# Softmax sums taken before the transposition, values as the stationary side: two attention layers of a four-layer kernel

## The reference, cut to what matters

```
x  = x + attention(q, k, v of norm(x), mask A) @ w_ao + b_ao     # self-attention
x  = x + attention(q of norm(x), k, v of ctx, mask B) @ w_co + b_co   # cross-attention
x  = x + gelu(norm(x) @ w1 + b1) @ w2 + b2                       # MLP, 256 -> 1024 -> 256

def attention(q, k, v, mask):                # 16 heads of 16 features, 64 keys
    scores = q k^T / 4
    scores = scores * mask - 10000 * (1 - mask)
    return softmax(scores) @ v
```

## Time and profile before

| what | us |
|---|---|
| median of 3 runs (lowest, highest) | 1135.61 (1134.04, 1136.98) |
| the profiled execution | 1134.52, of which 1132.7 between its first and last instruction |
| layer 0 and entry, up to the first `probs_T` | 120.8 |
| turn 0 | 68.9 |
| the six turns of the loop | 501.2 |
| turn 7, up to the next block's first matmul (L1620) | 74.2 |
| what follows (last MLP, layer 3) | 367.6 |

### The profile page before, as it was taken

The page is one execution under the profiler, slowest core; times in us unless marked ns, Lnnn a source line. Parts: engine busy times, 40 slices in busy tenths (PEclk is TensorE's granted clock), DMA queues, the critical chain, the costliest instruction groups (busy, mean ns, idle before and its releaser), DMA issues. The chain is left out here.

```text
span 1132.7 us, 23729 instructions
## 1 busy us (share of the span) xinstructions
PE 1030.0 (91%) x9056; PEld 707.2 (62%) x9056; DVE 768.0 (68%) x1517; ACT 517.4 (46%) x996; POOL 440.2 (39%) x387
## 2 busy tenths in 40 slices
PE   7988889999999999999999999998977978889766
PEld 5876666677777777678677677673453453544524
DVE  3655878856766766757757758744566796896854
ACT  4644354572572572662663663541404415314331
POOL 2111444443433433433443433523146356175240
PEclk9989889999999999999999999999989999999988
DMA  8130100001002002103001000300010010010100
GB/s 264 61 98 29 43 2 25 20 2 44 20 2 81 20 2 86 38 2 122 17 4 60 2 19 21 128 2 19 0 38 22 1 38 21 0 40 1 37 1 19
DMA packets 38005, 41.14 MB, mean 36 GB/s; under 512 B 8640, under 2 KB 33536, under 8 KB 37648
## 3 DMA queue, kind: packets, MB, share of 16 engines
q1 hardware_dynamic: 37776, 39.54, 10.9%
q0 software_dynamic: 128, 0.10, 0.1%
HBM read 31.25 MB, written 8.39 MB: 35 GB/s over the span
## 5 line engine op out<-in xcount | busy, mean ns | idle before, releaser
L2106 POOL TENSOR_TENSOR c_rs<-c_st,head_area 128x512 f32<-128x512 f32 x64 | 88.7, 1416 | 96.8 <-DVE c_st L2585 96.0
L787 POOL TENSOR_TENSOR head_area<-head_area,b_self_add 128x1024 f32<-128x1024 f32 x32 | 75.8, 2368 | 114.4 <-DVE head_area L1366 114.4
L1039 PE MATMUL ps<-b_hT_mlp,wl 128*128 128x512 f32 x224 | 107.0, 605 | 0.0
L787 POOL TENSOR_TENSOR head_area<-head_area 128x1024 f32<-128x1024 f32 x32 | 77.1, 2411 | 76.7 <-DVE head_area L1366 76.7
L1053 PE MATMUL ps<-w,b_act_g 128*128 128x256 f32 x448 | 100.9, 381 | 0.0
L1373 DVE TENSOR_REDUCE b_neg_max<-head_area 128x16 f32<-128x1024 f32 x64 | 77.5, 1211 | 34.1 <-POOL head_area L787 34.0
L1208 ACT ACTIVATE head_area<-head_area 128x1024 f32<-128x1024 f32 x64 | 67.9, 1061 | 62.6 <-DVE head_area L1378 62.5
L1213 ACT ACTIVATE head_area<-ps 128x512 f32<-128x512 f32 x128 | 69.8, 601 | 55.6 <-PE ps L986 55.6
L1053 PEld LDWEIGHTS ps<-w,b_act_g 128*128 128x128 f32 x448 | 83.4, 190 | 11.6 <-issue 1.0
L792 POOL TENSOR_TENSOR b_rstd<-b_var,minus_half 128x1 f32<-128x1 f32 x63 | 40.8, 648 | 124.9 <-DVE b_var L1402 124.2
L870 PE MATMUL ps<-head_area,wl 128*128 128x512 f32 x176 | 84.5, 609 | 3.9 <-issue 1.9
(11 more groups left out here) (262 smaller groups left out, 2155.9 us busy)
## 6 DMA issues: line engine op xcount, KB each, us to landing
head_area<-x_mid SPq DMA_DIRECT2D x9, 512.0 KB, 3.8
wl<-in_wl SPq DMA_DIRECT2D x4, 1024.0 KB, 7.0
head_area<-in_ctxT SPq DMA_DIRECT2D x8, 512.0 KB, 3.6
x_mid<-b_x_out SPq DMA_DIRECT2D x8, 512.0 KB, 3.5
area<-in_wc SPq DMA_DIRECT2D x1, 2336.0 KB, 8.2
a_x_in<-in_x SPq DMA_DIRECT2D x16, 128.0 KB, 2.9
a_y_in<-in_ctx SPq DMA_DIRECT2D x16, 128.0 KB, 3.6
w<-in_w SPq DMA_DIRECT2D x2, 1024.0 KB, 9.1
```

What stands on the lines that cost most here:

```text
L787: pool.tensor_tensor(t, t, m.unsqueeze(1).broadcast_to([P, NH, S]), ALU.add).then_inc(add_ok, 1)
L1039: mm = pe.matmul(ps[:, YB + j % 2, :], weight("w1", k, j * P, (j + 1) * P), hT_mlp[:, k, :], start=(k == 0), stop=(k == NC - 1))
L2106: pool.tensor_tensor(rs[:, i % BUFS, :], st[:, i % 3, :], rF[:, i // RS, :], ALU.mult).then_inc(rs_ok, 1)
```

## The change

- `row_sums` is new on DVE: a sum over 64 keys of the exponentials (128x1024) and a reciprocal, tile k + 1 in step k.
- `scale` is new on POOL: the probabilities times the reciprocals, 128x1024, in place; `probs_T` waits for it in place of `exps`.
- `times_v`: the values are the stationary side (128 keys x 32 columns, two heads) and the transposed probabilities move (64 columns). Four pairs of heads write four groups of 32 PSUM partitions. The result comes out transposed. The column of ones is gone (values are 32 wide instead of 34), and with it four memsets on POOL at the start.
- `normalize` (DVE) and `result_T` (PE) are removed.
- The order of a turn is new on PE, ACT, DVE and POOL.

```diff
+            def scale(n, k):
+                t = sc[:, k % 2, :, :, :].rearrange("q f i k -> q (f i) k")
+                pool.wait_ge(inv_ok, tile(n, k) + 1)
+                pool.tensor_tensor(t, t, inv_sum[:, k % 2, :].unsqueeze(2).broadcast_to([P, NH, S]), ALU.mult).then_inc(prob_ok, 1)
...
             def probs_T(n, k, nxt):
                 if k + 1 < TILES or nxt is not None:
                     pe.wait_ge(mul_ok, tile(n, k) + 2)
-                pe.wait_ge(exp_ok, tile(n, k) + 1)
+                pe.wait_ge(prob_ok, tile(n, k) + 1)
...
                 for half in range(2):
                     pe.wait_ge(pT_ok, 2 * tile(n, k) + half + 1)
-                    for i in range(NPAIR // 2):
-                        j = half * NPAIR // 2 + i
-                        for b in range(2):
-                            q = slice(b * S, (b + 1) * S)
-                            mm = pe.matmul(ps[q, CX, j * 2 * VW:(j + 1) * 2 * VW], pT[:, half, i, q], vP[a][:, 2 * p + b, j, :],
-                                           start=True, stop=True)
-                mm.then_inc(v_sum_ps, 1)
-
-            def result_T(n, k):
-                pe.wait_ge(tok_ok, tile(n, k) + 1)
-                for half in range(2):
-                    f = slice(half * P, (half + 1) * P)
-                    mm = pe.transpose(ps[:, CX, f], c_tok[:, f], w["ident"][:, :])
+                    for b in range(2):
+                        q = slice(b * S, (b + 1) * S)
+                        for i in range(NPAIR // 2):
+                            mm = pe.matmul(ps[i * PW:(i + 1) * PW, CX, half * P + b * S:half * P + (b + 1) * S], vP[a][:, 2 * p + b, half * NPAIR // 2 + i, :],
+                                           pT[:, half, i, q], start=True, stop=True)
                 mm.then_inc(c_ps, 1)
...
-            def normalize(n, k):
-
-                dve.wait_ge(v_sum_ps, tile(n, k) + 1)
-                heads = ps[:, CX, 0:NH * VW].rearrange("q (i v) -> q i v", v=VW)
-                dve.reciprocal(inv_sum[:, :], heads[:, :, HD:VW].rearrange("q i v -> q (i v)")).then_inc(inv_ok, 1)
-                dve.wait_ge(inv_ok, tile(n, k) + 1)
-                dve.tensor_tensor(c_tok[:, :].rearrange("q (i d) -> q i d", d=HD), heads[:, :, 0:HD],
-                                  inv_sum[:, :].unsqueeze(2).broadcast_to([P, NH, HD]), ALU.mult).then_inc(tok_ok, 1)
+            def row_sums(n, k):
+                t = sc[:, k % 2, :, :, :].rearrange("q b i k -> q (b i) k")
+                dve.wait_ge(exp_ok, tile(n, k) + 1)
+                dve.tensor_reduce(inv_sum[:, k % 2, :], t, AX, ALU.add).then_inc(sum_ok, 1)
+                dve.wait_ge(sum_ok, tile(n, k) + 1)
+                dve.reciprocal(inv_sum[:, k % 2, :], inv_sum[:, k % 2, :]).then_inc(inv_ok, 1)
...
             maximum(0, 0)
             subtract(0, 0)
             mask(0, 1)
+            row_sums(0, 0)
             turn(0, None, 1)
```

More of the change, by code:

```diff
@@ L34 @@
 NM = ROWS // HD
-VW = HD + 1
+PW = 2 * HD
 DFF = 1024
@@ L191 @@
 N_B_CONST = 4
-N_ZERO = 6
+N_ZERO = 2
 N_C_CONST = 11
@@ L321, in _ @@
                 pool.memset(w[a + "_v"][:, :, :, :], 0.0).then_inc(zero_ok, 1)
-            pool.wait_ge(zero_ok, 2)
-            for a in ("self", "cross"):
-                for odd in range(2):
-                    pool.memset(w[a + "_v"][odd * S:(odd + 1) * S, :, :, odd * VW + HD:odd * VW + VW], 1.0).then_inc(zero_ok, 1)
             pool.wait_ge(zero_ok, N_ZERO)
@@ L743, in _ @@
             store(5, rows[1])
-            sp.wait_ge(v_sum_ps, tile(TURNS - 1, NP))
+            sp.wait_ge(c_ps, tile(TURNS - 1, NP))
             for dst, src in load_c_weights(w, io):
@@ L804, in last_inv_std, with next_scale @@
                     inv_std(prev, TILES - 1)
+            def next_scale(n, k, nxt):
+                if k + 1 < TILES:
+                    scale(n, k + 1)
+                elif nxt is not None:
+                    scale(nxt, 0)
             def next_add_mask(n, k, nxt):
@@ L852, in _ @@
             add_mask(0, 1)
+            scale(0, 0)
             for p in range(NP):
@@ L1130, in turn @@
                 hidden(prev, 7, nxt)
-                last_project(n, 5, prev)
-                result_T(n, 5)
+                last_project(n, 6, prev)
                 probs_T(n, 6, nxt)
@@ L1137, in turn @@
                 next_scores(n, 6, nxt)
-                last_project(n, 6, prev)
-                result_T(n, 6)
                 mlp_out(prev, 0, nxt)
+                mlp_out(prev, 1, nxt)
                 probs_T(n, 7, nxt)
-                mlp_out(prev, 1, nxt)
                 last_project(n, 7, prev)
+                values_in(nxt, 1, prev)
                 times_v(n, 7)
-                values_in(nxt, 1, prev)
                 next_scores(n, 7, nxt)
@@ L1149, in turn @@
                 mlp_out(prev, 3, nxt)
-                result_T(n, 7)
             scores(0, 0)
@@ L1428, in next_subtract, with next_sums @@
                     subtract(nxt, 0)
+            def next_sums(n, k, nxt):
+                if k + 1 < TILES:
+                    row_sums(n, k + 1)
+                elif nxt is not None:
+                    row_sums(nxt, 0)
             def last_residual(n, k, prev):
@@ L1461, in turn @@
                 next_maximum(n, 1, nxt)
-                values(1, n, 1)
                 last_norm(n, 1, prev)
-                normalize(n, 1)
                 next_subtract(n, 1, nxt)
                 next_mask(n, 1, nxt)
-                stats_in(nxt if entry_of is None else entry_of)
-                last_residual(n, 2, prev)
-                next_mask(n, 2, nxt)
-                last_norm(n, 2, prev)
-                normalize(n, 2)
-                next_maximum(n, 2, nxt)
-                next_subtract(n, 2, nxt)
+                values(1, n, 1)
@@ L1476, in turn @@
+                next_sums(n, 1, nxt)
+                next_maximum(n, 2, nxt)
+                last_residual(n, 2, prev)
+                last_norm(n, 2, prev)
+                next_subtract(n, 2, nxt)
+                cross_masks(n)
+                next_mask(n, 2, nxt)
+                next_sums(n, 2, nxt)
+                stats_in(nxt if entry_of is None else entry_of)
+                last_residual(n, 3, prev)
                 next_maximum(n, 3, nxt)
+                next_subtract(n, 3, nxt)
@@ L1477, in turn @@
+                last_norm(n, 3, prev)
                 norm_in(nxt if entry_of is None else entry_of)
-                next_subtract(n, 3, nxt)
-                last_residual(n, 3, prev)
-                normalize(n, 3)
-                last_norm(n, 3, prev)
+                next_sums(n, 3, nxt)
                 next_mask(n, 3, nxt)
+                last_residual(n, 4, prev)
                 next_maximum(n, 4, nxt)
+                last_norm(n, 4, prev)
                 next_subtract(n, 4, nxt)
-                last_residual(n, 4, prev)
@@ L1509, in turn @@
-                normalize(n, 7)
+                next_mask(n, 7, nxt)
                 values(0, nxt, 1)
-                next_mask(n, 7, nxt)
                 result(prev, 2)
-                last_norm(n, 5, prev)
                 last_norm(n, 6, prev)
```

143 lines of the change are left out of this document (74 added, 69 removed).

## The result

The changed kernel takes 1138.92 us (median of 17 runs, 1133.45 to 1146.84) against 1135.04 (1129.38 to 1139.20) beside it: ratio 1.0043, interval 1.0022 to 1.0064. It is slower by some 4 us, less than half of the 9.4 forecast.

A forecast was written before the change was run, and what follows sets the result against it. PE's issue was taken to bound the loop, a tile's way through DVE, POOL and ACT turn 0. Terms +4.9 + 5.8 + 1 - 8.4 + 6.1 = +9.4 on 1134.5 gave 1143.9, as a median 1145 us; range 1118 to 1166.

The forecast's parts named there:

- The walk: Queues of a turn laid against each other at profiled lengths: loop turn 82.1 us, turn 0 74.7; chance 0.50 as it stands.
- The sign that the prediction had named: Granted clock falling in the new waits, which turn 0's rows (0.91) allow; it would show the prediction wrong.
- The reason given for the turn's length: Turn 0: no MLP fills PE, so a tile's way through DVE, POOL and ACT sets the pace; 74.7 for 68.9.
- PE waits 5 of its 6.3 us saved: Loop turn: PE rid of 6.3 us, 5 lost to waiting, so 82.1 for 83.5 and -8.4 over six turns.
- step 3: Fourth step of the walked loop turn: PE reaches `probs_T` 4 at 39.7, the tile at 40.5 us.
- PE and the tile are nearly level: Loop turn: PE and the scaled tile reach `probs_T` at nearly the same time in five of eight steps.
- the tile's way: From `scores` through mask, maximum, subtract, exp, sums and scaling to `probs_T`: 11.6 us for 7.6, 4.0 more per tile.
- The terms listed for the end of this turn: Turn 7: `probs_T` 7 at 70.3, then 0.9 + 0.9 + 0.6 + two `mlp_out` of 3.5, given as 80.3 us.
- its carried microsecond: End of turn 0: DVE about 1 us behind, counted as +1 in the sum.
- the fourth: Rival, loop turn: gains and losses cancel, PE waits 3.5 us a turn, not 5; 1136 us; chance 0.12.
- the first: Rival, loop: the tiles' way has room, PE stays packed, turns of 78 us; 1120, perhaps 1116; chance 0.19.
- The shared path: Rival: three more subtractions a turn begin under a `scale`, each +1.1 us, +3.4 a turn; 1172 us; chance 0.10.

The follow-up runs named there:

- e_nonorm: The changed kernel without the division (no `row_sums`, no `scale`; output not the reference's): 1125.5 us, ratio 0.990 to the kernel before.
- e_old_nonorm: The changed kernel without the division, all four engines in the order of before (no `result_T`, no `normalize`): 1099.0 us, ratio 0.970 to the kernel before.
- e_long: The changed kernel with `scale` reading its second operand as `add_mask` does, so it takes 2.36 us for 1.90: 1139.3 us, ratio 1.006 to the kernel before.

## Why the prediction was wrong in size

**The start**: +4.9 forecast, +4.4 measured. The term that was off is the scaling, 2.41 for 1.90; the queueing behind `add_mask` came as laid out (0.9 us).

**Turn 0**: 74.7 forecast, 78.1 measured. The walk left the clock out and said so; with the waits filled the turn is 74.3, and no step is more than 1.1 us from the walked one. But the sum then set this walk at full clock against a turn before that had itself lost to the clock (68.9, filled 66.2): like against like it would have been +8.5, and with both filled it is +8.1. The sign that the prediction had named, a granted clock that falls in the new waits, came: 0.81 for 0.91. The reason given for the turn's length stands less well. Not all is the division's: without any the turn is 74.6, against 63.8 in the old order. There PE waits at other places, as 4.27 us for a norm ahead of `times_v` 3 in e_nonorm:
```profile
152.46 0.69 PE L897 MATMUL ps<-ident,b_xc 128*128 128x128 f32 x2 [4.27 <-DVE b_xc L1378]
```

**The loop**: the step that failed. I walked a turn of 82.1 and -8.4 us over six; measured are 80.4 on average and -18.6. The failed step is that "PE waits 5 of its 6.3 us saved". What PE was rid of is 4.7 us a turn (83.5 to 78.8 in e_old_nonorm), not 6.3; of these it lost 1.6, not 5: 1.4 to waits of the new order (80.2 in e_nonorm), 0.90 of them at `queries_mid` 0, and some 0.2 to the division. Of the 4.7, `times_v` gave 8 x 0.48 = 3.8, as forecast; `result_T` and the waits around it gave the other 0.9, not 2.7, and where the rest went isn't shown.

Step by step, walked and measured (the median of the six loop turns): 9.5 / 10.1, 11.1 / 10.6, 10.0 / 9.8, 9.9 / 8.7, 11.5 / 11.1, 6.95 / 6.6, 11.35 / 11.1, 11.8 / 12.0. Two entries can be named. The wait of `queries_mid` 0 is 0.90, walked as 1.4. And step 3 was walked as 9.1 us of PE and 0.8 of waiting for the tile. It is 8.67 in the changed kernel, in e_long with a scaling of 2.36 and in e_nonorm with none: all of it is PE's own, and there was no wait. So the mis-sized scaling isn't the cause there; which of the queue's entries I laid too long isn't shown. The claim that PE and the tile are nearly level stood, for tiles 2 to 4; the inference that PE therefore loses what it saved did not, since being level costs nothing. Three of the six turns were below 80 us (79.4 to 79.95), which the prediction had named as a sign of being wrong.

**Turn 7**: +6.1 forecast, +5.2 measured, for the wrong reason. I put it to the tile's way, and it is as long without the division; what costs is the order, at a place where the next group's work is missing, and the lower clock behind it (0.94). With that place mended the turn is 76.7; what keeps it 2.5 us above the turn before isn't shown. The terms listed for the end of this turn, 70.3 + 0.9 + 0.9 + 0.6 + 7.0, also add up to 79.7 and not 80.3.

**The sum**: +4.4 + 9.2 - 18.6 + 5.2 + 0.3 = +0.5, and the profiled execution began turn 0 1.7 us later by chance (that point scatters over 9 us): +2.2, its own difference. The medians differ by 3.9, with an interval of 2.5 to 7.3 (0.22% to 0.64%). It was luck that the forecast of +9.4 came no further off: 10.2 too little gain in the loop and, its carried microsecond counted in, 2.4 too little loss in turn 0 partly cancel. Of the rivals, the fourth (1136) came nearest by number, with less waiting than walked; the first (PE stays packed) was nearer on the loop's waits and wrong in its sum of 78 a turn. The shared path came up once a turn, as at 126.18, and so it did before the change.

## What to carry to other kernels

Work moved off the bounding engine is worth its full time only in an order that has no waits of its own: here 36 us by the stages, of which the order that hides the new steps took 27 and the steps themselves 9. Ask of a new order what it does in the first and last turn, where the neighbour turns' work that covers its waits is missing, and give these turns places of their own. And when two queues are walked as level, that says that neither waits for long; it doesn't say that the slower of the two loses anything. Last, when a walk at full clock is set against a measured time, ask what the clock had cost that time.
